# A decoder layer on one core: ScalarE's wait for the last expert store moved behind the turned residual, and its first expert rows fetched ahead of the shared sums

## The reference, cut to what matters

```python
x = _layernorm(x + attn(x))     # a recurrence over time, 16 heads of 16x16 state
x = _layernorm(x + xattn(x, ctx))  # cross attention to 77 context rows, 16 heads
# ffn: 2 shared experts for every row, 8 routed experts of which each row takes the best 2
combine = sum(one_hot(top_idx) * softmax(gathered)[..., None])
shared_out = sum_n gelu(x @ Wfc_sh[n].T) @ Wproj_sh[n].T
routed_out = sum_e combine[e] * (gelu(x @ Wfc_r[e].T) @ Wproj_r[e].T)
x = _layernorm(x + shared_out + routed_out)
```

## Time and profile before

| | us |
|---|---|
| median of 3 runs | 2512.69 (2512.18 to 2513.38) |
| the profiled execution, its own time | 2510.64 |
| its span, first to last instruction | 2508.9 |
| TensorE busy / VectorE busy | 1775.7 / 2113.4 |
| ScalarE busy / POOL busy | 777.8 / 1022.5 |
| mean granted TensorE clock | 0.827 of full |

### The profile page before, as it was taken

The page is one execution under the profiler, slowest core; times in us unless marked ns, Lnnn a source line. Parts: engine busy times, 40 slices in busy tenths (PEclk is TensorE's granted clock), DMA queues, the critical chain, the costliest instruction groups (busy, mean ns, idle before and its releaser), DMA issues.

```text
span 2508.9 us, 32575 instructions
## 1 busy us (share of the span) xinstructions
PE 1775.7 (71%) x9438; PEld 1345.3 (54%) x9438; DVE 2113.4 (84%) x5985; ACT 777.8 (31%) x2209; POOL 1022.5 (41%) x1164
## 2 busy tenths in 40 slices
PE   4258887888788878887888430367786568857884
PEld 2135666667566666666667420245574436745673
DVE  5999999899999999999899989999998979941000
ACT  2142145313631363146313100252223511234121
POOL 2503350364246414641474467353653653230103
PEclk7558998999799979998989765668898679976997
DMA  8000342325232423342324220000363003630243
GB/s 265 19 1 25 112 135 73 108 99 173 68 111 100 170 76 104 111 158 76 103 97 164 84 88 8 20 1 3 101 202 122 18 1 108 203 126 1 97 157 116
DMA packets 175116, 238.57 MB, mean 95 GB/s; under 512 B 28657, under 2 KB 148074, under 8 KB 174954
## 3 DMA queue, kind: packets, MB, share of 16 engines
q1 hardware_dynamic: 140874, 194.46, 23.2%
q10 hardware_dynamic: 27936, 25.44, 3.2%
q0 software_dynamic: 6144, 16.79, 2.1%
HBM read 202.09 MB, written 33.16 MB: 94 GB/s over the span
## 4 chain that ended last, share of the span: by engine, by line
PE 46%; DVE 22%; ACT 11%; POOL 9%; issue 6%; DMA 5%; ACTq 1%; SPq 0%; POOLq 0%; PEldq 0%; DVEq 0%
PE ps L629 11%; PE ps L620 9%; PE ps L573 7%; PE ps L566 6%; ACT probs L820 4%; DVE ps L1544 4%; DVE ps L1525 4%; DVE prod L1517 3%; DVE terms L1532 2%; DMA pj<-in_wpT 2%; ACT hT L899 2%; PE ps L422 2%; PE ps L523 2%; DMA out_rows<-y 2%; DVE terms L1527 1%
## 5 line engine op out<-in xcount | busy, mean ns | idle before, releaser
L1544 DVE TENSOR_REDUCE ps<-terms 128x64 f32<-128x320 f32 x1024 | 448.3, 483 | 0.0
L1525 DVE TENSOR_REDUCE ps<-prod 128x16 f32<-128x272 f32 x1024 | 396.9, 432 | 0.0
L620 PE MATMUL ps<-xg,fc 128*128 128x128 f32 x2848 | 362.2, 289 | 29.6 <-PE ps L629 12.4
L1532 DVE TENSOR_TENSOR terms<-ps,rec_out 128x256 f32<-128x256 f32 x1024 | 381.0, 413 | 0.0
L1517 DVE TENSOR_TENSOR prod<-ps,rec_in 128x256 f32<-128x256 f32 x1024 | 380.7, 413 | 0.0
L620 PEld LDWEIGHTS ps<-xg,fc 128*128 128x128 f32 x2848 | 351.4, 204 | 52.6 <-issue 44.1
L629 PE MATMUL ps<-pj,hT 128*128 128x256 f32 x1424 | 338.1, 391 | 34.7 <-ACT hT L899 34.7
L629 PEld LDWEIGHTS ps<-pj,hT 128*128 128x128 f32 x1424 | 268.1, 193 | 89.6 <-ACT hT L899 55.1
L1132 POOL TENSOR_TENSOR oprod<-SE_out,rec_q 128x320 f32<-128x320 f32 x171 | 147.5, 862 | 349.3 <-DVE SE_out L1536 348.7
L566 PE MATMUL ps<-xtf,fc 128*128 128x512 f32 x512 | 243.3, 614 | 3.4 <-ACT vec L785 3.4
L573 PE MATMUL ps<-pj,hT 128*128 128x256 f32 x1024 | 240.0, 386 | 0.0
(11 more groups left out here) (227 smaller groups left out, 2872.1 us busy)
## 6 DMA issues: line engine op xcount, KB each, us to landing
fc<-in_wfcT SPq DMA_DIRECT2D x80, 1024.0 KB, 5.2
pj<-in_wpT SPq DMA_DIRECT2D x80, 1024.0 KB, 8.3
xg_rows<-in_rows ACTq DMA_DIRECT2D x105, 128.0 KB, 2.1
out_rows<-y ACTq DMA_DIRECT2D x89, 128.0 KB, 5.7
in_rows<-o_rows SPq DMA_DIRECT2D x2, 2176.0 KB, 17.4
out_rows<-o_rows SPq DMA_DIRECT2D x2, 2176.0 KB, 17.0
xtp<-in_xT SPq DMA_DIRECT2D x32, 128.0 KB, 2.5
xin<-in_x SPq DMA_DIRECT2D x8, 512.0 KB, 7.0
```

Source lines behind the costliest of these rows:

```text
L620: i = mm(ps[:, UP + g // 4, g % 4 * P:(g % 4 + 1) * P], fc[:, par, c, g * P:(g + 1) * P], xg[:, c], start=c == 0, stop=c == KC - 1)
L1525: red(SE[:, old, cols, HD:EH].rearrange("p v n -> p n v"), prod[:, c % PLACED, :, cols, 0:HD + 1], AX.X, ALU.add).then_inc(step_done, 1)
L1532: tt(terms[:, cols, :, 0:NV], SE[:, old, cols, HD:EH].unsqueeze(2).to_broadcast([P, HC, HD, NV]), rec_out[:, c].unsqueeze(1).to_broadcast( ...
L1544: red(SE[:, new, cols, 0:HD], terms[:, cols, :, 0:NV + 1], AX.X, ALU.add).then_inc(step_done, 1)
```

## The change

Two things change, both in ScalarE's stream; no other engine's code is touched.

- **The wait for the last store.** `last_experts` no longer ends with `all_stored`. It returns the count, and in periods 1 to 4 the router calls `all_stored` between the two copies of the turned residual and the wait for the router's scores. In period 5, which has no router, it stands where it was. For the bound tiles 5 and 6 it moves from the end of their own period to the next one, behind the copies of `project_rows`; for tile 7 it is called at the very end.
- **The first rows.** The wait for the scatter and the load of the first 128 rows now come right behind the second shared expert's last Gelu, then the nine bounds, then the wait for the turned rows, the copy to `xg` and the load of the second 128 rows, and only then the two copies of `sums`.

```diff
--- before.py
+++ after.py
@@ -834,8 +834,9 @@
                     act.wait_ge(spread_ps, m * 2 + (c + 1))
                     fn(xtf[:, c], ps[:, ACC + c, :], ACT.Copy).then_inc(spread_sb, 1)
 
-            def router(m):
+            def router(m, between):
                 out_of_banks(x2T, x2T_ps, x2T_sb, m)
+                between()
                 act.wait_ge(rt_ps, m + 1)
                 fn(rt[:, :, :].rearrange("g b e -> g (b e)"), ps[:, A0, 0:B * 2 * NR], ACT.Sigmoid).then_inc(rt_sb, 1)
 
@@ -871,16 +872,17 @@
 
             def first_rows(m, lo):
 
-                act.wait_ge(scattered, (m + 1) * (MOVES * 16))
-                act.dma_start(xg_rows[:, :], in_rows[m % 2][0:P]).then_inc(xg_in, 16)
                 rows_turned(m, lo + (m + 1))
                 act.dma_start(xg_rows[:, :], in_rows[m % 2][P:2 * P]).then_inc(xg_in, 16)
 
             def routed_experts(m, experts, before=()):
 
                 if experts[0] == NSH:
+                    act.wait_ge(scattered, (m + 1) * (MOVES * 16))
+                    act.dma_start(xg_rows[:, :], in_rows[m % 2][0:P]).then_inc(xg_in, 16)
                     load_bounds(m)
                     first_rows(m, bounds_of_tile[m][NSH][0])
+                    sums(m)
                 bounds_of = bounds_of_tile[m]
                 base = bounds_of[NSH][0]
                 for i, e in enumerate(experts):
@@ -920,12 +922,11 @@
 
             def last_experts(f, between):
                 if f is not None:
-                    all_stored(routed_experts(f, EXPERTS[LATE:], between))
-                else:
-                    for part in between:
-                        part()
-
-            def period(p, m=None, f=None, bound=False, preps=Q, upcoming=None, begun=False, begin=False):
+                    return routed_experts(f, EXPERTS[LATE:], between)
+                for part in between:
+                    part()
+
+            def period(p, m=None, f=None, bound=False, preps=Q, upcoming=None, begun=False, begin=False, stored=None):
 
                 def prep(q):
                     if q < preps:
@@ -936,6 +937,8 @@
                         prep(0)
                     if bound:
                         project_rows(m - FIRST_BOUND)
+                        if stored is not None:
+                            all_stored(stored)
 
                 def attend():
                     if m is not None:
@@ -960,22 +963,23 @@
                     if not bound:
                         prep(2)
 
-                last_experts(f, (start, attend, weigh, lambda: None, second))
+                hi = last_experts(f, (start, attend, weigh, lambda: None, second))
                 if m is not None:
-                    router(m)
+                    router(m, lambda: all_stored(hi) if f is not None else None)
+                elif f is not None:
+                    all_stored(hi)
+                if m is not None:
                     shared(m, 0, lambda: weights(m))
                     if bound:
                         prep(2)
                     shared(m, 1)
-                    sums(m)
                 if upcoming is not None and not bound:
                     gate_rows(upcoming - FIRST_BOUND)
                 if m is not None:
                     own = EXPERTS[NSH:] if bound else EXPERTS[NSH:LATE]
                     ahead = [lambda: None] * (len(own) - 1) + [lambda: prepare((p + 1) * R + 1)]
                     hi = routed_experts(m, own, ahead if begin else ())
-                if bound:
-                    all_stored(hi)
+                return hi
 
             act.sem_inc(sh_gelu, 2)
             act.sem_inc(acc_sb, 1)
@@ -991,9 +995,9 @@
                 period(p, p, p - 1)
             period(4, 4, 3, begin=True)
             period(5, None, 4, upcoming=5, begun=True)
-            period(6, 5, bound=True, upcoming=6, begin=True)
-            period(7, 6, bound=True, preps=CH, upcoming=7, begun=True)
-            period(8, 7, bound=True, preps=0)
+            hi = period(6, 5, bound=True, upcoming=6, begin=True)
+            hi = period(7, 6, bound=True, preps=CH, upcoming=7, begun=True, stored=hi)
+            all_stored(period(8, 7, bound=True, preps=0, stored=hi))
 
 
         @block.gpsimd
```

## The result

The kernel after took 2480.92 us (median of 4 runs, 2477.74 to 2483.78), the kernel before beside it 2512.43 (4 runs, 2511.10 to 2513.38): the ratio is 0.9876, with a 95% interval from 0.9862 to 0.9889. That is 31.5 us less, where 36.0 were forecast; 2480.9 lies inside the range. The profiled execution after took 2477.74 with a span of 2476.0, so between the two profiles 32.9 us are to be found (2508.9 less 2476.0).

The account below looks back on a forecast made before the run. VectorE was taken as held at fixed places by the TensorE and ScalarE path. Free stretch 19.6, tile 6 6.8, tile 7 6.1 and its first rows 3.5 make 36.0 us: 2476.7, range 2467 to 2486 (over the cases 2464 to 2494).

Parts of the forecast that it names:

- Rival (d): Free stretch: waits only change place and the tail alone moves, 9.6 us, giving 2503.1 us; chance 0.05.
- The router: Periods 1 to 4: copies before the store wait; TensorE gains 5.0 us, `rt` comes 4.1 us earlier in tile 1.
- Rival (e): Router: a 1.4 us drain behind the table load, so `rt` gains 2.7 us, not 4.1; 2478.1 us; chance 0.06.
- The free stretch: 230 to 1330 us, before period 5: of VectorE's 28.1 us of waits, 21.8 go; 19.6 kept after POOL.
- POOL's step in period 4: End of period 4: POOL's combine 19.7 us early, VectorE 21.8; 2.2 us return as a wait at the last norm.
- Rival (b): After the first tile, POOL or the out store holds VectorE; tiles 2 to 4 give nothing: 2488.7 us; chance 0.13.
- Tile 6: Period 5 onward: tile 6's projected rows, 6.78 us late to VectorE behind a copy awaiting a store, give 6.8 us.
- Tile 7's projected rows: Behind the recurrence: copies follow the turn, 4.2 us, and projection at 2.4 GHz, another 1.9: 6.1 us.
- The first rows: Shared experts' end, every tile: early load leaves TensorE's register loads, taken as 4.9 us; gain 3.5 us per tile.
- rival (a): First rows: TensorE's register loads fill its idle time; tiles 0 and 7 lose 3.5 us each: 2483.7 us; chance 0.15.
- The sums: Behind the second load of rows: 1.1 us of copies hidden by TensorE's first half of an up.
- rival (c): `sums`, awaiting the output's landing, holds the first Gelu: 40 us lost in 8 tiles, 2516.7 us; chance 0.03.

Follow-up runs that it names:

- experiment 4: Changed kernel plus nine extra matmul calls on constants in period 8, keeping TensorE busy before tile 7's turn: 2478.32 us, ratio 0.9862.
- (6): Changed kernel with the copies of `sums` ahead of the first rows' turn, behind the load and the bounds: 2480.70 us, ratio 0.9869.
- experiment 5: Changed kernel once more, unchanged, beside the last three kernels: 2483.19 us, ratio 0.9879.
- experiments 3: Changed kernel with TensorE's nine register loads ahead of the second shared expert instead of behind it: 2474.54 us, ratio 0.9843.
- experiment 7: Changed kernel with TensorE's nine register loads behind the issue of the shared experts' last down matmuls: 2474.83 us, ratio 0.9849.
- experiment 8: Changed kernel with register loads behind the last down matmuls, nine extra matmuls before tile 7's turn, sigmoid table loaded before the moved wait: 2472.90 us, ratio 0.9836.
- experiment 1: Changed kernel with only the waits for the last store moved; first rows and sums in the old order: 2495.88 us, ratio 0.9929.
- experiment 2: Changed kernel with only first rows, bounds and sums in the new order; `all_stored` as before the change: 2499.15 us, ratio 0.9948.

## Why the prediction was right, and where not

- **What bounded the kernel** was right. VectorE's waits at fixed places were the time to be won, and they went from 28.1 to 8.3 us. Rival (d), that the waits only change place, is refuted by the 20.9 us won before period 5.
- **The router** was right in each step: TensorE without its idle, scores in 1.96 us, the table load open, `rt` 2.3 us late (forecast 2.6). Rival (e), a drain behind the table load, is refuted by 0.02 us between load and sigmoid. By the Trainium skill (ScalarE: Activation LUTs, What ACT_TABLE_LOAD costs) some 1380 ns of drain belong to the switch; the trace agrees with its 1283 ns for the load and shows no such drain: not before the sigmoid, ahead of which ScalarE had idled 4.65 us, nor at the Gelu, whose load began 0.02 us behind the sigmoid and whose first activation came 0.01 us behind the load.
- **The free stretch** was right in size: 19.6 forecast, 20.9 in the profiled execution. Of the 20.9 some 1.4 are no part of the change, for tile 0's router output was ahead by as much already (L549 at 220.39 instead of 221.76). Four executions with both edits in it gave 20.9, 18.5 (experiment 4), 17.8 (6) and 15.9 (5), so 19.6 is at the upper side. The cap by the first minimum shows in ScalarE's new wait (8.1 us), and in experiments 3 and 7, where the wait grew to 22.7 and 29.3 us and VectorE's lead at the end (15.7 and 19.1 us) was no larger than these.
- **POOL's step in period 4** was right, though VectorE's wait for `y_out` kept its 1.8 us. VectorE was to be 21.8 us early there and POOL 19.7. At the first routing reduce VectorE was 23.6 us early (22.2 without the 1.4 us named above), and POOL, with 1.4 us of its idle time gone, 20.9 (19.5 without the 1.4 that stood before the stretch). The forecast looked for the difference as a wait; 2.7 us of it went into VectorE's small routing instructions instead, which ran beside POOL's products. The three that grew most ended within 0.04 us of the end of one of these (L1368 at 1223.91, POOL's at 1223.87). In experiment 8, where all but one kept their length, the difference came out as the wait of 5.30 us. Rival (b), which would have stopped the gain after tile 1, is refuted: VectorE's lead at the first routing reduce was 10.1, 13.6, 17.4 and 23.6 us in periods 1 to 4. Its mechanism holds at the end of period 4.
- **Tile 6** was right: 7.0, forecast 6.8.
- **Tile 7's projected rows** are the term that failed: 2.7 us (3.3 in experiment 5) instead of 6.1. The failed step is "as TensorE hardly idles, the projection should run at 2.4 GHz". The forecast moved everything behind the turn and left what stands before it alone, though its own other terms brought TensorE to this place earlier than VectorE's gated rows. The idle doubled, from 2.48 to 4.90 us, and the turn (1.94, not 1.07) and the projection (6.25, not 3.5) ran at 1.2 GHz. Where the idle was 2.80 us (experiment 1) or filled (experiment 4), the projection took 3.72, near the forecast 3.5.
- **The first rows** were right in mechanism, and rival (a) is refuted, since some of the idle did go. But TensorE's nine loads take 6.3 us, not 4.9: the idle fell by 2.05 us in tile 7, not 3.5. The step that failed is ScalarE's pace as a stand-in for TensorE's. It wasn't needed: the prediction, and rival (a) with it, says that no row shows TensorE's loads, and the trace of the kernel before has them (L596, at 0.65 us each, over some 6.1 us behind the shared experts' end). Beyond that idle the tail can't be read finely: experiment 1, whose idle before L602 stayed at 8.39 us, ended 1.9 us earlier in the tail too.
- **The sums** were right: they lie hidden behind TensorE's work, and rival (c) is refuted; `out_stored` holds ScalarE no more than 1.8 us in the free stretch. What the forecast didn't see is how much the second edit protects the first: it was priced at 3.5 us in tile 0 and again in tile 7, and experiment 1 shows that without it most of the router's gain in the free stretch is lost.

The sum: 36.0 less 3.4 for tile 7 and 1.2 for the tail, and 1.3 more in the free stretch, is 32.7; tile 6's 0.2 makes 32.9. That the total comes so near owes something to luck: 1.4 of these 32.9 us are no part of the change, and the profiled execution is the shortest of its kernel. **Open** is why executions of the changed kernel lie up to 5 us apart at the end of the free stretch. Between the profile after and experiment 5 it can be said where: 0.9 us stood before 230 us, and 1.7 came at tile 3's quotient, where VectorE waited 1.60 us for ScalarE in experiment 5 and not at all in the other. No run here was made for the cause.

## What to carry to other kernels

When a wait is moved off the path, go on to the next place where the same engine meets something paced by the slower path: here the gain of the first edit was lost at the output store until the loads no longer stood behind it. An engine made earlier idles longer at its next meeting, and may come out of it at half its clock, so its later work has to be priced with the new idle and not with the old. Nine register loads are no small thing beside a 0.7-us turn: put them where queued matmuls cover them.

## What was not expected of the hardware

- TensorE's nine register loads took 0.30 us each (median) and began 0.65 us apart; they and what follows held it for 6.3 us where none ran long. ScalarE's nine took 0.28 us each and began 0.54 us apart (535.7 to 540.0 in tile 1 of the kernel before). Issued while 7.07 us of matmuls were queued, TensorE's left 2.2 to 2.9 us open (experiment 7).
- VectorE's smallest routing instructions (128x8, 1x9 and 128x32 elements) took 0.44, 0.32 and 0.19 us in period 4 of the kernel before and 1.72, 1.12 and 1.28 in the kernel after, where POOL's products of 128x512 ran at that time. No run here was made for the cause.
- The eight transposes of tile 7's turn took 1.06 us in experiment 1, where TensorE had idled 2.80 us before them, 1.94 in experiment 2 (3.02 of idle), 1.31 in experiment 5 (4.69) and 1.94 in the kernel after (4.90). The clock so lost didn't come back with work: in the last two the projection's 16 matmuls took 6.43 and 6.25 us, with no more than 0.7 us of idle before them.
